# The lower halves of the attention's probabilities: subtracted on DVE instead of POOL

## What is computed

```python
scores = jnp.einsum('bhqd,bhkd->bhqk', q, k) / jnp.sqrt(jnp.float32(HEAD_DIM))
scores = jnp.where(causal, scores, -jnp.inf)
attn = jax.nn.softmax(scores, axis=-1)
ctx = jnp.einsum('bhqk,bhkd->bhqd', attn, v)
...
x = x + _L1_attn_ref(_layernorm(x), ...)
x = x + 0.5 * _L1_ffn_ref(_layernorm(x), ...)
```

## Time and profile before

| | us |
|---|---|
| median of 3 runs | 2859.77 |
| lowest and highest | 2859.61, 2860.03 |
| profiled execution | 2863.14 |
| its span, first to last instruction | 2861.2 |
| DVE busy | 1953.1 (68%) |
| POOL busy | 1074.0 (38%) |
| L2039 on POOL, 176 times | 351.3 |
| L1781 on DVE, 176 times | 156.2 |

### The profile page before, as it was taken

The page is one execution under the profiler, slowest core; times in us unless marked ns, Lnnn a source line. Parts: engine busy times, 40 slices in busy tenths (PEclk is TensorE's granted clock), DMA queues, the critical chain, the costliest instruction groups (busy, mean ns, idle before and its releaser), DMA issues.

```text
span 2861.2 us, 55968 instructions
## 1 busy us (share of the span) xinstructions
PE 2420.5 (85%) x23228; PEld 1837.5 (64%) x23228; DVE 1953.1 (68%) x3305; ACT 1687.1 (59%) x2898; POOL 1074.0 (38%) x823
## 2 busy tenths in 40 slices
PE   2777787877898988889898988899988888889888
PEld 1455555655676776667575766666765667767667
DVE  7688788988687876767678667678776772434432
ACT  2255566555767766566666565666664565547554
POOL 0144445543343533153535353444444352122112
PEclk9799999999999999999898989999998899999999
DMA  3100000000000000000000000000000000000000
GB/s 126 46 1 1 1 1 1 1 1 1 1 1 1 1 1 10 15 13 13 13 13 13 13 13 13 12 13 13 13 12 21 9 1 8 8 8 1 8 8 8
DMA packets 34843, 32.90 MB, mean 11 GB/s; under 512 B 7648, under 2 KB 33952, under 8 KB 34592
## 3 DMA queue, kind: packets, MB, share of 16 engines
q1 hardware_dynamic: 34592, 29.33, 3.1%
HBM read 12.28 MB, written 4.19 MB: 6 GB/s over the span
## 4 chain that ended last, share of the span: by engine, by line
PE 52%; DVE 25%; ACT 9%; POOL 6%; issue 6%; SPq 1%; DMA 1%; DVEq 0%; POOLq 0%; ACTq 0%
PE psum L625 13%; PE psum L627 12%; PE psum L626 12%; PE psum L631 4%; PE psum L1057 2%; PE psum L1059 2%; PE psum L1058 2%; DVE a1pr L1781 2%; POOL f1hT L2052 2%; POOL a1pr L2039 2%; PE psum L908 2%; DVE a1c L1799 1%; DVE f1e L1892 1%; PE psum L961 1%; DVE a1nm L1758 1%
## 5 line engine op out<-in xcount | busy, mean ns | idle before, releaser
L2052 POOL TENSOR_TENSOR f1hT<-f1g,f1hT 128x512 f16<-128x512 f32 x256 | 304.8, 1197 | 791.5 <-ACT f1hT L1447 791.0
L2039 POOL TENSOR_TENSOR a1pr<-a1PT,a1pr 128x1024 f16<-128x1024 f32 (+1 forms) x176 | 351.3, 1999 | 293.5 <-DVE a1pr L1781 293.5
L625 PE MATMUL psum<-f1sl,f1w1h 128*128 128x256 f16 x1024 | 287.8, 281 | 16.8 <-ACT f1g L1442 8.6
L625 PE MATMUL psum<-f1w2h,f1hT 128*128 128x256 f16 x1024 | 280.1, 273 | 11.5 <-POOL f1hT L2052 9.1
L626 PE MATMUL psum<-f1sl,f1w1h 128*128 128x256 f16 x1024 | 287.0, 280 | 0.0
L627 PE MATMUL psum<-f1sl,f1w1l 128*128 128x256 f16 x1024 | 286.7, 280 | 0.0
L627 PE MATMUL psum<-f1w2h,f1hT 128*128 128x256 f16 x1024 | 279.1, 273 | 0.0
L626 PE MATMUL psum<-f1w2l,f1hT 128*128 128x256 f16 x1024 | 279.1, 273 | 0.0
L1758 DVE TENSOR_REDUCE a1nm<-psum 128x2 f32<-128x768 f32 (+3 forms) x176 | 198.2, 1126 | 78.0 <-PE psum L888 77.2
L1781 DVE CAST a1pr<-a1PT 128x1024 f16<-128x1024 f32 (+1 forms) x176 | 156.2, 892 | 86.4 <-ACT a1PT L1343 67.1
L625 PE MATMUL psum<-wguh,f0xT 128*128 128x352 f16 x512 | 164.9, 322 | 42.7 <-DVE f0xT L1605 14.2
(11 more groups left out here) (336 smaller groups left out, 7434.9 us busy)
## 6 DMA issues: line engine op xcount, KB each, us to landing
a1Q<-a1st SPq DMA_DIRECT2D x96, 64.0 KB, 2.6
a1K<-a1st SPq DMA_DIRECT2D x96, 64.0 KB, 2.6
x<-in_L_attn_x SPq DMA_DIRECT2D x8, 512.0 KB, 8.8
out<-x SPq DMA_DIRECT2D x8, 512.0 KB, 2.9
wslot<-in_L_ffn_w SPq DMA_DIRECT2D x1, 1024.0 KB, 7.7
wraw<-in_L_ffn_w SPq DMA_DIRECT2D x1, 1024.0 KB, 5.6
wslot<-in_L_ffn_slot_embeds SPq DMA_DIRECT2D x1, 1024.0 KB, 7.8
a1Q<-a1mr SPq DMA_DIRECT2D x64, 4.0 KB, 1.7
```

What stands on the lines that cost most here:

```text
L625: e.matmul(out, lh, rh, start=start, stop=False)
L2039: e.tensor_tensor(a1["pr"][:, i % 2, 1, :, 0:w], a1["PT"][:, i % 2, :, 0:w], a1["pr"][:, i % 2, 0, :, 0:w], ALU.subtract).then_inc(s["a1_pl"])
L2052: e.tensor_tensor(hT1[:, 1, 2 * hp:2 * hp + 2, :], gg[:, hp % 2, :, :], hT1[:, 0, 2 * hp:2 * hp + 2, :], ALU.subtract).then_inc(s["f1_hl"])
```

## The change

The subtraction goes from POOL's stage `a1_probs`, which is taken away, into DVE's stage of that name. It stands in the same part as the cast, so nothing can be put between the two, and it waits for the cast's semaphore `a1_ph`. Operands, sizes, buffers and what the others wait for (`a1_pl`) stay as they are.

```diff
@@ vector, a1_probs
-                        e.tensor_copy(a1["pr"][:, i % 2, 0, :, 0:w], a1["PT"][:, i % 2, :, 0:w]).then_inc(s["a1_ph"])
+                        pr, PT = a1["pr"][:, i % 2, :, :, 0:w], a1["PT"][:, i % 2, :, 0:w]
+                        e.tensor_copy(pr[:, 0, :, :], PT).then_inc(s["a1_ph"])
+                        q.wait_ge("a1_ph", i + 1)
+                        e.tensor_tensor(pr[:, 1, :, :], PT, pr[:, 0, :, :], ALU.subtract).then_inc(s["a1_pl"])
@@ gpsimd
-            def a1_probs(b):
-                S = at_a1(b)
-                for c in range(2):
-                    for g, (t, j0, n) in enumerate(A1_GROUPS):
-                        i = (2 * b + c) * NG + g
-                        yield S + a1_s2_at(c, g) + 2.8
-                        w = n * (t + 1) * P
-                        q.wait_ge("a1_ph", i + 1)
-                        e.tensor_tensor(a1["pr"][:, i % 2, 1, :, 0:w], a1["PT"][:, i % 2, :, 0:w], a1["pr"][:, i % 2, 0, :, 0:w],
-                                        ALU.subtract).then_inc(s["a1_pl"])
-
```

More of the change, by code:

```diff
@@ L2055, in gpsimd @@
             return [weights(), *[chain(z, 2 * B) for z in (f0_powers, f0_products, f0_hidden, f0_halves)],
-                  *[chain(z, B) for z in (a0_powers, a0_values, a1_powers, a1_probs)],
+                  *[chain(z, B) for z in (a0_powers, a0_values, a1_powers)],
                   *[chain(z, 2 * B) for z in (f1_powers, f1_mlp)]]
```

## The result

| | before | with the change |
|---|---|---|
| median, us | 2859.4 | 2866.2 |
| ratio, 95% interval | | 1.0025 (1.0016 to 1.0034) |
| profiled execution, us | 2863.1 | 2864.5 |
| its span, us | 2861.2 | 2862.7 |

The change made the kernel a quarter of a per cent slower. The forecast was 0.9% faster, with a chance of 0.19 for slower. The two profiled executions lie on opposite sides of their medians and are only 1.4 us apart, so from here on executions explain where time goes, and medians say how much. They also hide one difference: PE's mean granted clock was 0.942 and 0.941 in them, but 0.944 on the mean of 72 runs of the kernel before and 0.938 on the mean of the 16 runs of the changed one, none of which lay above 0.941.

A forecast was written before the change was run, and what follows sets the result against it. No engine alone was taken as the bound: PE's fixed order is held up by short waits. The chain's terms -61 - 19 + 45 + 7 + 1 gave -27 us, -25 was taken: 2835 us, range 2806 to 2870.

The forecast's parts named there:

- What bounds the kernel: Whole kernel: no engine alone is the bound; PE works in fixed order, held up by short waits; POOL's subtraction stalls DVE.
- Parts 1 and 2: Attention stretch's chain: subtraction leaving POOL's 45.7 us for 26 on DVE gives -19 us; DVE stalls that go give -61.
- rival (b): Attention stretch: freed stalls are covered by other waits, no change within 0.2%, 2860 us; chance 0.14.
- Part 3: DVE in the attention stretch: subtractions of 1.225 and 0.96 us; 43 of 54 chain casts get one inserted, +45 us.
- Part 4: Attention stretch: POOL's remaining L2052 still contends with DVE's new subtraction, 0.1 us for each of 66 on the chain, +7 us.
- Part 5: All engines' newly planned order: reshuffle nothing in sum, a lottery of several us; ACT's 8 more table loads +1 us.
- The sum: Whole kernel: -27 us by the chain, -17 by PE's waits; -25 taken, giving 2835 us, 0.9% faster.
- The second way: PE's waits in the attention stretch: freed 19, 7 and perhaps 2 us, other DVE waits +11, giving -17 us.
- The guess that PE's clock had room to rise: PE in the attention stretch: granted clock, mean 0.93, can rise where idle time goes; not in the sum.
- (a): Attention stretch: DVE becomes the bound, slower; each further cast on the chain costs 1.04 us, 48 give 2883 us; chance 0.19.
- the four lines whose doubled waits were listed as a sign of being wrong: PE's waits behind DVE lines L1758, L1841, L1917 and L1888: if they double, the forecast is wrong.

The follow-up runs named there:

- six plans for the same work: Planner's durations for cast and subtraction scaled by 0.96 to 1.06, against the table as it is: POOL 2810.6 to 2878.1 us, DVE 2829.7 to 2866.2 us.
- the fastest plan for POOL: Kernel before, subtraction still on POOL, planned with cast and subtraction 4% dearer than in the table: 2810.6 us, ratio 0.9826.

## Why the prediction was wrong, point by point

**What bounds the kernel:** right that waits in PE's order and not an engine's load set the time, and that POOL's subtraction stalls DVE. The experiment without subtraction confirms the second with 73 us.

**Parts 1 and 2, what is freed (61 us of stalls and 46 us of POOL's step, 107 in all): this is the step that failed.** The stalls were real and they went, but each microsecond that they had on the chain was counted as a microsecond of time. In the order of before only 73 us came free (70 to 84 by the ratio's interval), 34 less than the prediction had. Those 34 us are nearly the whole way from the forecast of about -27 us to the +7 measured in that order. In place of the freed pieces PE's own work stood on the chain, 771 us where it had 624. Which wait took over at which place was not followed. That is the overlap that rival (b) describes.

**Part 3, what DVE gets:** the durations are right (1248 ns for 1225; 1073 for 0.96 us with 768, somewhat short). The count is wrong. "43 of the 54 casts go on to other DVE work" took the chain of before as the chain after; with 23 steps that had been POOL's that made 66 subtractions on the chain. With the same order 116 were on it, and in the changed kernel 35, at nearly the same time. The whole price of the insertion, 45 + 26 + 7 = 78 us in the prediction, was 80 all the same: 116 instances at 0.69 us each instead of 66 at 1.18. That is two errors that cancel, and so luck.

**Part 4, contention that stays:** right, small: 23 ns above 1225 for 1024 elements, 0.11 us for 768, 0.1 us taken. The other way round POOL's L2052 went from 1200 to 1269 ns on the mean in the stretch.

**Part 5, the order:** named "a lottery of several us" and priced at nothing. For this one plan the net was indeed -1 us (2867.3 in the old order, 2866.2 in the new one), but by luck, in two ways. First, it is the sum of two larger effects. Taking for each kernel the product of PE's busy time and clock in its profiled execution, and the mean clock of its runs, I estimate that the new order took 12 us off PE's idle time (451 to 439) and added 11 to its busy time (2414 to 2425), since the clock fell from 0.944 to 0.938. Second, among six plans for the same work the time ran over 68 us on POOL and over 37 on DVE. That is more than the whole forecast and it should have been the width of the range: the range of 2806 to 2870 did hold the time, by 4 us, but the weight of 0.67 on "faster" left the plan's scatter out.

**The sum:** -27 by the chain and -17 by PE's waits missed the same thing. The second way let the waits on other DVE lines grow "by a fifth, +11", a fraction for which no row stands. In the old order they grew by 30, from 57 to 87 us, which is the +28 that rival (b) had named. In the changed kernel they grew by 5 only, to 63, but the waits on ACT, for which the sum had nothing, grew by 32, from 37 to 69: the new order changed the kind of wait and not the outcome. The guess that PE's clock had room to rise where idle time goes fits the run without the subtraction (0.952 on the mean of its runs, with zeros in PE's operands) and was wrong for the change (0.938, where it had been 0.944).

**The rivals:** (a) has the right sign and the wrong price. With 62 more pairs on the chain its own formula (-27 + 62 x 1.04) gives about 2897 us, 30 too high, and in the changed kernel the chain did not move onto DVE at all. (b) has the mechanism, waits that cover what was freed, and its time of 2860 is 6 us off. Of the four lines whose doubled waits were listed as a sign of being wrong, L1758's went from 14.1 to 38.0 us and L1917's from 2.6 to 5.1; L1841's fell from 13.8 to 0.5 and L1888's rose from 2.6 to 3.4 only.

**What stays open:** the mean effect of the move over plans (-0.43%, 0.81 to either side), and why exactly one plan beats another. That a plan for POOL suits both kinds of work and a plan for DVE only DVE's was shown on two orders each.

## What to carry to other kernels

The length of the pieces that leave a chain of waits is not yet the gain: here 107 us on the chain gave 73, because other work stood ready to take their place on it. Nor does the chain of before tell the price of what is added: 66 new instances were counted on it, 116 were on the chain of one order and 35 on that of another, at the same time. Where a list scheduler sets the order, any edit is also a new draw: before judging an edit, time it in the old order, and time old and new under a few meaningless changes to the planner's numbers; the scatter between plans (here 0.8% for POOL's and 0.5% for DVE's) is the error bar. Look at PE's clock beside its idle time, since they can move against each other and hide both. Trying such draws can be worth more than an edit: the best plan for the unchanged work is 1.7% faster than the kernel before, seven times what the change itself moved.

## What the runs showed of the hardware

POOL's elementwise operation stopped a small DVE operation with two SBUF operands for what was left of its length: 2.12 us for 0.29 us of work in the earlier trace rows, ending 0.15 us behind POOL's. With POOL's subtraction gone the median of that operation fell from 894 to 292 ns. The subtraction as a whole, with these stalls, held 73 us of the time of an otherwise unchanged order, although DVE had 314 us to spare in the same stretch. The order alone also moved PE's clock: the same 23228 matmuls were busy for 2391.8 us at a mean granted clock of 0.955 in the fastest plan for POOL, and for 2420.5 at 0.942 in the plan of before. With the same order and the work on DVE instead of POOL, the mean clock of the runs stayed at 0.944; with the new order it was 0.938.
